# Weighting the expert rows in the last step: diagonal fp32 products on TensorE in place of multiply-adds on three engines

## The reference, cut to what matters

```
normed = layernorm(x) * gamma + beta
probs  = softmax(normed @ router_w.T)           # 8 experts
top_v, top_i = top_k(probs, 2)
gates  = softmax(top_v)                         # two weights a token
out    = sum over the 2 chosen experts e of gates[e] * swiglu(normed, gate_up_w[e], down_w[e])
out    = out + swiglu(normed, shared_gate_up_w, shared_down_w)
x      = x + tanh(g_ffn[1]) * out
```

## Time and profile before

| | us |
|---|---|
| median of 3 runs | 320.44 (320.19 to 322.36) |
| the profiled execution, whole | 319.61 |
| its span, first to last instruction | 317.8 |
| TensorE busy | 268.3 (84%) |
| VectorE busy | 236.4 (74%) |
| ScalarE busy | 204.4 (64%) |
| GpSimd busy | 158.9 (50%) |
| mean granted TensorE clock | 0.941 of 2.4 GHz |

### The profile page before, as it was taken

How to read it: one execution, slowest core, us unless ns; L and a number is a source line. 1 busy time by engine, 2 the same in 40 slices (tenths; PEclk the granted TensorE clock), 3 DMA queues, 4 the chain that set the end, 5 groups by cost and what they waited for, 6 DMA issues and landing times.

```text
span 317.8 us, 7526 instructions
## 1 busy us (share of the span) xinstructions
PE 268.3 (84%) x2406; PEld 201.9 (64%) x2406; DVE 236.4 (74%) x711; ACT 204.4 (64%) x469; POOL 158.9 (50%) x206
## 2 busy tenths in 40 slices
PE   7878986997999797999988853878899999999950
PEld 4553442555677464676766732368799999999940
DVE  3586198857977666788999967998576767677796
ACT  2964799796577588976855543535657575756560
POOL 2624297024622546643024777770047878787531
PEclk9999999899999999999999655879999999999995
DMA  7890003001269999970000011113122223111064
GB/s 211 233 383 10 1 2 132 0 3 19 117 188 185 178 181 180 190 105 0 2 1 24 30 45 40 53 49 88 37 71 68 78 67 87 51 32 33 8 226 132
DMA packets 34612, 28.12 MB, mean 88 GB/s; under 512 B 3072, under 2 KB 32389, under 8 KB 33936
## 3 DMA queue, kind: packets, MB, share of 16 engines
q1 hardware_dynamic: 32192, 23.77, 33.8%
q0 software_dynamic: 2240, 3.72, 3.6%
q10 hardware_dynamic: 144, 0.15, 0.2%
HBM read 14.15 MB, written 14.40 MB: 90 GB/s over the span
## 4 chain that ended last, share of the span: by engine, by line
PE 52%; DVE 30%; ACT 8%; issue 6%; DMA 2%; SPq 1%; POOL 1%; DVEq 0%
PE bank L1195 47%; DVE region_k L912 2%; DVE region_x L1152 2%; DVE top L911 2%; DMA wr<-in 2%; PE bank L1492 1%; DVE bn_raw L870 1%; DVE nm L1001 1%; DVE region_k L1003 1%; DVE x L1141 1%; DVE x L1142 1%; ACT x_hat L540 1%; DVE x L902 1%; PE bank L1419 1%; DVE region_k L969 1%
## 5 line engine op out<-in xcount | busy, mean ns | idle before, releaser
L1177 DVE TENSOR_TENSOR region_k<-region_x,region_k 128x768 f16<-128x768 f32 (+1 forms) x33 | 30.6, 926 | 21.6 <-ACT region_k L714 21.6
L1195 PE MATMUL bank<-w_high,region_k 128*128 (+1 forms) x380 | 37.8, 221 | 6.4 <-DVE x L1171 3.3
L1195 PE MATMUL bank<-w_scaled,w_high 128*128 128x256 f16 x252 | 42.5, 273 | 0.1
L846 POOL DMA_INDIRECT expert_rows<-region_k,slot_dest x22 | 27.1, 1232 | 26.5 <-DVE region_k L1164 19.2
L714 ACT ACTIVATE region_k<-region_x 128x768 f16<-128x768 f32 (+1 forms) x33 | 26.8, 813 | 15.8 <-DVE region_x L1152 13.7
L820 POOL DMA_INDIRECT dispatched_rows<-region_t,slot x28 | 28.8, 1028 | 16.1 <-issue 8.3
L1195 PEld LDWEIGHTS bank<-w_high,region_k 128*128 128x128 f16 x380 | 30.9, 99 | 7.7 <-issue 7.3
L1195 PE MATMUL bank<-w_scaled,w_low 128*128 128x256 f16 x126 | 34.3, 273 | 0.0
L1195 PE MATMUL bank<-w_low,region_k 128*128 (+1 forms) x190 | 34.0, 221 | 0.0
L1152 DVE SCALAR_TENSOR_TENSOR region_x<-bank,region_w 128x768 f32<-128x768 f32 (+1 forms) x33 | 30.4, 920 | 3.2 <-ACT region_w L719 2.2
L1195 PE MATMUL bank<-filler 128*128 128x512 f16 x94 | 26.9, 407 | 3.9 <-DVE region_k L912 2.4
(11 more groups left out here) (242 smaller groups left out, 736.1 us busy)
## 6 DMA issues: line engine op xcount, KB each, us to landing
dispatched_rows<-pad_rows SPq DMA_DIRECT2D x8, 1048.0 KB, 18.8
w_scaled<-in SPq DMA_DIRECT2D x5, 1024.0 KB, 8.0
w_scaled<-dispatched_rows SPq DMA_DIRECT2D x21, 131.0 KB, 2.3
region_q<-expert_rows SPq DMA_DIRECT2D x3, 512.0 KB, 5.0
x<-in SPq DMA_DIRECT2D x4, 256.0 KB, 4.4
region_w<-in SPq DMA_DIRECT2D x2, 512.0 KB, 7.0
out<-x SPq DMA_DIRECT2D x3, 256.0 KB, 2.3
w_scaled<-in SPq DMA_DIRECT2D x1, 704.0 KB, 4.1
```

The lines of the kernel that those rows point to most:

```text
L846: pool.indirect_dma_start(ytok, bass.IndirectOffsetOnAxis(dst[:, n, h:h + 1].bitcast(U32), 0), yv[n % 4][:, h * D:(h + 1) * D], None, boun ...
L1177: dve.tensor_tensor(hsplit[:, v, k:2 * k], hid[:, v, 0:k], hsplit[:, v, 0:k], ALU.subtract).then_inc(hidden_low, 1)
L1195: return pe.matmul(o, l, r, start=start, stop=stop)
```

## The change

ScalarE makes 24 diagonal matrices while the steps run: `ident` times `gate[:, t, c]` for the 12 tiles of groups 0 to 2 and both weights, 128x128 in fp32. One is made after the Silu of each of the iterations 8 to 23 and two in each of 24 to 27 (`DIAGONAL_AT`). They lie in `xh` and in `region_s`, which nothing reads any more by then. TensorE multiplies each diagonal with its 128x128 block of `yk` in fp32, two products a tile summed in one quarter of a bank (`weigh`): group 2 into bank 6 in iteration 31, behind `down(30)`; group 0 into bank 0 in iteration 32, behind `down(31)`; group 1 into bank 1 behind `down(32)`. VectorE adds a whole bank to four tiles of `x` with one tensor_tensor (`add_weighted`). Group 3 stays multiply-adds, now on VectorE (`sum_rows(3)`, four instructions). ScalarE's 12 multiplications and GpSimd's 4 additions are gone. The loads are issued in the order 2, 3, 0, 1, the stores in the order 2, 3, 4, 0, 1.

```diff
--- before.py
+++ after.py
@@ -57,9 +57,13 @@
 GROUP_OF_LAST = {hi - 1: g for g, (lo, hi) in enumerate(GROUPS)}
 TURN_BANK = ((6, 7), (6, 7), (6, 7), (0, 1), (4, 5))
 DENSE_FIRST = 3
+WEIGHTED = (2, 0, 1)
 STEPS = [("shared", b) for b in range(B)] + [("dense", e) for e in range(DENSE_FIRST)] + [("rows", n) for n in range(TILES)] + [("dense", e) for e in range(DENSE_FIRST, E)]
 STEP_OF = {n: s for s, (kind, n) in enumerate(STEPS) if kind == "rows"}
 LAST_ROWS = STEP_OF[TILES - 1]
+DIAGONALS = [(t, c) for t in range(3 * T) for c in range(2)]
+DIAGONAL_AT = {STEP_OF[1] + i: DIAGONALS[i:i + 1] for i in range(16)}
+DIAGONAL_AT.update({STEP_OF[17] + i: DIAGONALS[16 + 2 * i:18 + 2 * i] for i in range(4)})
 GATE_BANK = {0: 2, 1: 0, 2: 4}
 EARLY = 12
 AT_ONCE = 3
@@ -288,6 +292,7 @@
         dst = sb("slot_dest", [P, TILES, 2], I32)
         xdt = wf[:, 8 * PAY_W:8 * PAY_W + 2 * TP].bitcast(F16).rearrange("p (r n) -> p r n", r=2)
         sil = region_w[:, 0:2 * HB].rearrange("p (r n) -> p r n", r=2)
+        diag = [xh[:, :, :], region_s[:, :].bitcast(F32).rearrange("p (t d) -> p t d", d=D)]
         hid = xf[:, 0:2 * HB].rearrange("p (r n) -> p r n", r=2)
         hsplit = region_k[:, 0:3, :].rearrange("p a b -> p (a b)").bitcast(F16).rearrange("p (r n) -> p r n", r=2)
         xt_ps = bank[6][:, 0:TP].bitcast(F16)
@@ -438,9 +443,9 @@
         rows_ready = sem("rows_ready")
         rows_sent = [sem(f"rows_sent{r}") for r in range(4)]
         sum_done = sem("sum_done")
-        last_gated = sem("last_gated")
         gates_done = sem("gates_done")
-        last_added = sem("last_added")
+        gate_diagonals = sem("gate_diagonals")
+        rows_weighted = sem("rows_weighted")
 
         def columns(s):
             return S if STEPS[s][0] == "shared" else HB
@@ -455,6 +460,8 @@
         def up_ps(s):
             c = gate_up_bank(s) * 512 + columns(s)
             return psum[:, c:c + columns(s)]
+
+        SUM_BANK = 3 - gate_up_bank(len(STEPS) - 1)
 
         def wait(eng, s, v):
 
@@ -514,11 +521,11 @@
             for r in range(4):
                 eng.wait_ge(rows_sent[r], 32 * len(range(r, TILES, 4)))
 
-            for g in (0, 2, 1, 3):
+            for g in (2, 3, 0, 1):
                 n = slice(*GROUPS[g])
                 eng.dma_start(yk[:, n, :], ytok_v[:, n, :]).then_inc(x_loaded[g], 16)
-            for g, ready, count in ((2, last_added, 2), (0, sum_done, T), (SPARSE, rows_ready, len(STEPS)), (3, last_added, 4),
-                                    (1, sum_done, 2 * T)):
+            for g, ready, count in ((2, sum_done, 1), (3, sum_done, 2), (SPARSE, rows_ready, len(STEPS)), (0, sum_done, 3),
+                                    (1, sum_done, 4)):
                 n = slice(*GROUPS[g])
                 eng.wait_ge(ready, count)
                 eng.dma_start(out_v[:, n, :], x[:, n, :]).then_inc(stored, 16)
@@ -722,15 +729,12 @@
                 if s == 0:
                     act.wait_ge(top2_difference, 1)
                     act.activation(gone[:, :], gdif[:, :], ACT.Tanh, scale=0.5).then_inc(top2_tanh, 1)
-
-            act.wait_ge(gates_done, 1)
-            for g in (2, 3):
-                act.wait_ge(x_loaded[g], 32)
-                for c in range(2):
-                    for t in range(*GROUPS[g]):
-                        last = act.activation(yk[:, t, c * D:(c + 1) * D], yk[:, t, c * D:(c + 1) * D], ACT.Copy,
-                                              scale=gate[:, t, c:c + 1])
-                    last.then_inc(last_gated, 1)
+                for t, c in DIAGONAL_AT.get(s, ()):
+                    if (t, c) == (0, 0):
+                        act.wait_ge(gates_done, 1)
+                        act.wait_ge(ffn_low, len(GROUPS))
+                    act.activation(diag[c][:, t, :], ident, ACT.Copy, scale=gate[:, t, c:c + 1]).then_inc(gate_diagonals, 1)
+
 
         @block.gpsimd
         def _(pool):
@@ -846,13 +850,6 @@
                     pool.indirect_dma_start(ytok, bass.IndirectOffsetOnAxis(dst[:, n, h:h + 1].bitcast(U32), 0),
                                             yv[n % 4][:, h * D:(h + 1) * D], None,
                                             bounds_check=2 * B * S - 1, oob_is_err=False).then_inc(rows_sent[n % 4], 16)
-
-            for k, (g, c) in enumerate(((2, 0), (2, 1), (3, 0), (3, 1))):
-                n = slice(*GROUPS[g])
-                pool.wait_ge(last_gated, k + 1)
-                if c == 1:
-                    pool.wait_ge(last_added, k)
-                pool.tensor_tensor(x[:, n, :], x[:, n, :], yk[:, n, c * D:(c + 1) * D], ALU.add).then_inc(last_added, 1)
 
         @block.vector
         def _(dve):
@@ -1135,12 +1132,23 @@
                 dve.scalar_tensor_tensor(dst[:, n, :], xd[:, n % 4, :, D + 1], te[:, n:n + 1], xd[:, n % 4, :, D],
                                          ALU.is_equal, ALU.add).then_inc(dest_ready, 1)
 
-            def sum_rows(tiles_of_group):
-
-                for t in tiles_of_group:
-                    link(dve.scalar_tensor_tensor(x[:, t, :], yk[:, t, 0:D], gate[:, t, 0:1], x[:, t, :], ALU.mult, ALU.add))
-                    dve.scalar_tensor_tensor(x[:, t, :], yk[:, t, D:2 * D], gate[:, t, 1:2], x[:, t, :], ALU.mult,
-                                             ALU.add).then_inc(sum_done, 1)
+            def add_weighted(g, o):
+
+                n = slice(*GROUPS[g])
+                dve.wait_ge(rows_weighted, WEIGHTED.index(g) + 1)
+                dve.tensor_tensor(x[:, n, :].rearrange("p t d -> p (t d)"), x[:, n, :].rearrange("p t d -> p (t d)"),
+                                  bank[o][:, :], ALU.add).then_inc(sum_done, 1)
+
+            def sum_rows(g):
+
+                dve.wait_ge(x_loaded[g], 32)
+                for c in range(2):
+                    for t in range(*GROUPS[g]):
+                        last = dve.scalar_tensor_tensor(x[:, t, :], yk[:, t, c * D:(c + 1) * D], gate[:, t, c:c + 1], x[:, t, :],
+                                                        ALU.mult, ALU.add)
+                    if c == 0:
+                        link(last)
+                last.then_inc(sum_done, 1)
 
             for s in range(len(STEPS) + 2):
                 v = s % 2
@@ -1178,13 +1186,11 @@
                                       ALU.subtract).then_inc(hidden_low, 1)
                 if ahead[0] == "rows" and ahead[1] < 2:
                     slot_dest(ahead[1])
-                if s == len(STEPS) - 1:
-                    dve.wait_ge(x_loaded[0], 32)
-                    sum_rows(range(0, 1))
-                elif s == len(STEPS):
-                    sum_rows(range(1, 4))
-            dve.wait_ge(x_loaded[1], 32)
-            sum_rows(range(4, 8))
+                if s == len(STEPS):
+                    add_weighted(2, 6)
+                    sum_rows(3)
+            add_weighted(0, SUM_BANK)
+            add_weighted(1, SUM_BANK + 1)
 
         @block.tensor
         def _(pe):
@@ -1547,6 +1553,15 @@
                         last = mm(o, lo, w[i][0], False, i == len(w) - 1)
                 last.then_inc(down_made, 1)
 
+            def weigh(g, o):
+
+                pe.wait_ge(x_loaded[g], 32)
+                pe.wait_ge(gate_diagonals, len(DIAGONALS))
+                for u, t in enumerate(range(*GROUPS[g])):
+                    for c in range(2):
+                        last = mm(bank[o][:, u * D:(u + 1) * D], diag[c][:, t, :], yk[:, t, c * D:(c + 1) * D], c == 0, c == 1)
+                last.then_inc(rows_weighted, 1)
+
             gate_up(0, None)
             first = STEP_OF[0]
             e = before = None
@@ -1582,7 +1597,13 @@
                     turn(ahead[1])
                 elif s > 0:
                     down(s - 1, expert_of(s - 1))
+                if s == len(STEPS) - 2:
+                    weigh(2, 6)
+                elif s == len(STEPS) - 1:
+                    pe.wait_ge(hidden_done, len(STEPS) - 1)
+                    weigh(0, SUM_BANK)
             down(len(STEPS) - 1, None)
+            weigh(1, SUM_BANK + 1)
 
 
 def constants():
```

## The result

| | before | after |
|---|---|---|
| median of 20 runs each, us | 321.32 | 318.91 |
| ratio, 95% interval | | 0.9937 (0.9909 to 0.9965) |
| the profiled execution: whole, span | 319.61, 317.8 | 318.32, 316.4 |
| VectorE / ScalarE / GpSimd busy | 236.4 / 204.4 / 158.9 | 231.8 / 207.7 / 155.1 |
| TensorE busy | 268.3 | 273.7 |

The change makes the kernel faster by 0.6% (0.35 to 0.9%), 2.0 us; the medians differ by 2.4. Forecast were 2.4 us, 318.0, in a range of 316.6 to 320.8.

What follows compares the result with a forecast made beforehand. VectorE was taken to bound the tail, then TensorE: its products end at 311.85, the last addition at 312.6, plus 2.77 gives 315.35 against 317.8. Taking 2.4 off the median 320.44 gives 318.0, range 316.6 to 320.8.

Steps and rivals of the forecast that it cites:

- Part 1, what is removed: In the tail: ScalarE's 3.66 us, GpSimd's 4.27 and VectorE's slow stretch (some 3 us lost) go, none on the new path.
- Part 2, the diagonals: ScalarE, iterations 8 to 27: 24 more multiplications fit into its waits after the Silu; cost zero, 7.4 us at most.
- rival 5: A diagonal is late and TensorE waits for ScalarE, though the last is made 15 us ahead; chance 1%.
- Part 3, the loads: Loads issued from 300.0: group 2 lands at 303.9, group 3 about 304.7, group 0 about 306.2, group 1 at 307.8.
- Rival 3: Group 2's load, first in the queue, lands later and TensorE's tail loses 1.5 us: median 319.5; chance 9%.
- Part 4, the products: TensorE's tail: fp32 `weigh` blocks of 1.89 us, 0.118 an instruction, between the `down` blocks, ending at 311.85.
- The sum: Span end 315.35 against 317.8: 2.4 us less, 0.8%, giving a median of 318.0.
- The waits: VectorE idles from 305.61 while `down(31)` is 1.5 us late, then waits half a microsecond before its last addition.
- A sign of being wrong that came: The prediction called itself wrong if, among other signs, the steps before 300 us in the trace had moved.
- rival 1: TensorE's clock falls to 1.2 GHz in the tail: median 322.8 from `weigh(0)` on, 325.7 from 304 on; chance 6%.
- rival 2: TensorE's fp32 weight loads, 0.195 us each, are not hidden: 3.7 us more, median 321.7; chance 6%.
- rival 4: Tail shorter than worked out: pace 0.109, last store and waits another half microsecond less; median 317.0; chance 14%.

Runs made afterwards that it cites:

- half the products: The changed kernel without the second weight's product of the 12 tiles: 317.40 us, ratio 0.9899 to before; tail (first expert-row load's issue to span end) 13.3 us.
- group 3 early: The changed kernel with VectorE's four multiply-adds of group 3 moved into iteration 32: 319.49 us, ratio 0.9883 to before, tail 15.1 us.
- the sums all on VectorE: The kernel before with groups 2 and 3 also summed by VectorE, no other engine taking part: 320.39 us, ratio 1.0005 to before, tail 16.7 us.
- The repeat: The changed kernel measured again, nothing altered: 318.91 us beside 320.17 before, ratio 0.9942, tail 15.1 us.
- the kernel with the last store from ScalarE: The changed kernel with group 3 early, tiles 6 and 7 on VectorE, group 1's store split, its last half from ScalarE's queue: 317.60 us, ratio 0.9931 to before.
- the split store's kernel: The changed kernel with group 3 early, tiles 6 and 7 summed on VectorE and group 1 stored in two halves: 319.27 us, ratio 0.9767 to before.
- the first run with two tiles on VectorE: The changed kernel with group 3 early and tiles 6 and 7 of group 1 summed by VectorE: 318.16 us, ratio 0.9864 to before, tail 14.2 us.

## Why the prediction was right

- **What bounds.** TensorE takes VectorE's place in the tail; shown from both sides, by half the products (tail 1.8 shorter) and by group 3 early (no change).
- **Part 1, what is removed.** The 3 us lost to GpSimd were measured by themselves at 3.0 us. They are not the gain: the new path has 7.75 us of TensorE where VectorE's was cleared, and with the sums all on VectorE only 1.1 us of tail came back.
- **Part 2, the diagonals.** Zero, to 0.01 us over 71.48. The gaps were 0.78 and 0.5; about 0.7 and, for two, 1.07 - 0.70 = 0.37 were worked out. The 0.39 of one instruction overlaps the Silu before it by 0.10. The last diagonal was dated wrongly: 288.6 is behind the Silu one iteration earlier, and in the changed kernel the last one ended at 292.7. That is still 12 us ahead of the first product, so nothing hung on it and rival 5 did not come.
- **Part 3, the loads.** The first landed 3.83 us after its issue (3.9), and no other was waited for. Rival 3, a late first load, did not come: in all eight traces in which TensorE waited for the first load, it began 3.67 to 3.94 us after the issue.
- **Part 4, the products.** 1.89, 1.84 and 1.84 us a block (1.89). The row at 38.63 was the right one to take: 5.57 us for the 24 products against 5.66 forecast. Within a block a product took 0.22 us against 0.236; what the block has on top is its first product, 0.33 and 0.28. The Trainium skill (FP8 and Floating Point Precision, TensorE Precision Notes) gives true fp32 four passes; the estimate from it, 0.22 us a product, is met within a block.
- **The sum.** A tail of 15.35 from an issue at 300.0 was forecast, 15.1 measured. TensorE began 0.1 us sooner after the issue than worked out and its stretch was 0.1 shorter. The last addition and the 2.8 us behind it were as worked out.
- **The waits.** VectorE was to wait half a microsecond ahead of its last addition and did, 0.64. `down(31)` held back cost it 1.37 us (about 1.5 worked out). The prediction asks for six blocks without gaps but lists five, and five came.
- **The level.** 318.0 was the forecast, 318.91 the median: the kernel before had 321.32 over 20 runs and not the 320.44 of the three shown. The difference of medians is 2.4 as forecast, the ratio says 2.0. That the medians agree to a tenth is in part luck, since the interval of the ratio reaches from 1.1 to 2.9 us.
- **A sign of being wrong that came.** The prediction calls itself wrong if the steps before 300 have moved, and in the first trace the loads came 1.26 us late. The repeat has them at 299.79, and from iteration 8 to the loads both kernels take 71.5 us, so the change did not move them.
- **The rivals.** The clock stayed at 1.00 until after 314, so rival 1 did not come. The weight loads did not set the pace (rival 2): 0.11 us an instruction against their 0.195. Of rival 4 the pace within a block came, 0.11 against 0.118, but not the half microsecond at the last store: landings of stores were 2.3 to 2.8, a little longer than before.

## What to carry to other kernels

When work moves to an idle engine, price the chain that the new engine makes, not the one that it clears. Here a 3 us slowdown was removed, and the kernel gained 2.0 us by its ratio and 2.7 in the tail. TensorE's 5.6 us of products cost that little because they partly fill time in which it waited before (0.84 and 1.52 us), and because VectorE's chain could shrink beside them. In a tail of a few microseconds compare traces from one fixed event to the end; whole times scatter by more than the effect. Even there split the tail once more, at the end of the last engine: the kernel with the last store from ScalarE met its forecast by the tail, though at most 0.2 of the 0.5 us came from the store. After such a move look at once for the engine that now waits: VectorE's 2.5 us of idle time could take back two tiles, and the next bounds were the last load, with 0.26 to 0.34 us of waiting in three of four traces, and the last store.

## What the runs showed of the hardware that was not expected

The loads were issued anywhere from 297.7 to 303.3 us into the span, with the same instructions ahead of them up to the diagonals. The granted clock of TensorE differs between the executions there. Stretches of TensorE (stretch, length, busy, clock, DMA share, GB/s) of the split store's kernel, loads at 297.73:

```profile
5.00:50.00 45.00, 37.63 (x229) 1.00 0.39 128
50.00:75.00 25.00, 20.42 (x179) 1.00 0.13 43
160.00:222.00 62.00, 45.19 (x389) 0.78 0.14 42
```

and of the first run with two tiles on VectorE, loads at 303.34:

```profile
5.00:50.00 45.00, 37.55 (x218) 0.96 0.37 127
50.00:75.00 25.00, 20.95 (x155) 0.93 0.13 43
160.00:222.00 62.00, 47.23 (x381) 0.75 0.12 37
```

All thirteen traces, by the mean clock of these three stretches (between 75 and 160 it is 1.00 in all of them):

| clock 5 to 50 | 50 to 75 | 160 to 222 | loads issued |
|---|---|---|---|
| 1.00 | 1.00 | 0.78 | 297.73 |
| 1.00 | 0.93 | 0.78 | 299.79, 299.84, 300.0 |
| 1.00 | 0.93 | 0.75, 0.72 | 300.81, 300.88 |
| 0.96 | 1.00 | 0.78 | 300.82, 301.26, 301.37 |
| 0.89 | 1.00 | 0.78 | 301.52, 302.80 |
| 0.96 | 0.93 | 0.78, 0.75 | 302.36, 303.34 |

The one without a fall to the lower level ahead of 160 is the earliest of all; those with falls in both early stretches are among the latest. The kernel before (300.0) and the changed one (301.26) stand in different rows, and the changed one again (299.79) stands in the row of the kernel before. So the 1.26 us goes with the clock's course, not with the change. That the clock is the cause, and not a companion, was not tried; if it is, it moves the loads by up to 5.6 us, more than twice what the change gains.
